# Layer norms applied by ScalarE with scale and bias, and the high half of a transposed mixing rounded straight from PSUM, in a four-layer graph stack

## The reference

```
h = max(layernorm(x), 0);  x = x + L0(h, adj)   # hypergraph: D^-1 H B^-1 H^T (h W1^T) + b1, relu, a layer norm
                                                # over 1024 with gamma and beta, then the same with W2, b2
h = max(layernorm(x), 0);  x = x + L1(h, adj)   # three times adj @ (h W) + b, relu after the first two
h = max(layernorm(x), 0);  x = x + L2(h, adj)   # attention transition T from two scores; relu(sum_k T^k h Wk + bk)
h = max(layernorm(x), 0);  x = x + L3(h, adj)   # relu([h, adj h / degree] W^T)
layernorm(x) = (x - mean) / sqrt(var + 1e-5)
```

## Time and profile before

| | |
|---|---|
| runs | 2774.39 us, median of 3 (2774.32 to 2774.5) |
| profiled execution, span from its first to its last instruction | 2775.4 us |
| around the span | nothing that the profile shows; the median of the runs is 1.0 us shorter |
| PE, PEld busy | 2708.2 us (98%), 2255.6 (81%) |
| DVE, ACT, POOL busy | 2130.3 us (77%), 977.0 (35%), 1219.8 (44%) |
| 16 groups of layer 0, 1, 2, 3 | up to about 945, 1670, 2330 us and the end |

### The profile page before, as it was taken

One profiled execution on the slowest core, in us unless ns is written; L12 is line 12 of the kernel. 1 busy time (PEld: TensorE's weight loads), 2 busy tenths in 40 slices (PEclk: granted clock), 3 DMA queues, 4 the chain that ended last, 5 costly groups with the idle time before them and its releaser, 6 DMA issues.

```text
span 2775.4 us, 42799 instructions
## 1 busy us (share of the span) xinstructions
PE 2708.2 (98%) x13410; PEld 2255.6 (81%) x13410; DVE 2130.3 (77%) x4696; ACT 977.0 (35%) x1905; POOL 1219.8 (44%) x1463
## 2 busy tenths in 40 slices
PE   6999999999999999999999999999999999999999
PEld 4888878888788788888888887888888887888887
DVE  6888888888888766666666668888888887777776
ACT  3334333343333445555554552222222222121221
POOL 4433444343443667677676773211211213333332
PEclk9999999999999999999999999999999999999999
DMA  4111111111111311111111122111111112233232
GB/s 129 41 36 43 38 36 40 36 45 36 36 39 40 95 48 57 41 56 47 51 49 53 49 78 67 53 55 53 53 55 53 53 55 86 87 90 94 80 94 76
DMA packets 126793, 161.26 MB, mean 58 GB/s; under 512 B 53408, under 2 KB 53408, under 8 KB 126752
## 3 DMA queue, kind: packets, MB, share of 16 engines
q1 hardware_dynamic: 121856, 151.84, 17.6%
q10 hardware_dynamic: 4896, 8.92, 1.1%
HBM read 93.60 MB, written 67.11 MB: 58 GB/s over the span
## 4 chain that ended last, share of the span: by engine, by line
PE 84%; DVE 7%; issue 3%; POOL 3%; ACT 2%; DMA 0%; SPq 0%; DVEq 0%; ACTq 0%; POOLq 0%
PE ps L388 25%; PE ps L390 24%; PE ps L389 24%; PE ps L404 4%; PE ps L417 3%; PE ps L406 2%; DVE col_lo L729 1%; DVE normed L756 1%; POOL col_lo L1067 1%; DVE stats L737 1%; DVE wide L875 1%; DVE row_lo L729 1%; ACT row_hi L574 0%; ACT col_hi L574 0%; POOL w_lo L1067 0%
## 5 line engine op out<-in xcount | busy, mean ns | idle before, releaser
L388 PE MATMUL ps<-w_hi,col_hi 128*128 128x512 f32 x3072 | 1233.0, 401 | 24.7 <-DVE col_lo L729 16.3
L390 PE MATMUL ps<-w_hi,col_lo 128*128 128x512 f32 x3072 | 1200.7, 391 | 0.0
L389 PE MATMUL ps<-w_lo,col_hi 128*128 128x512 f32 x3072 | 1197.7, 390 | 0.0
L388 PEld LDWEIGHTS ps<-w_hi,col_hi 128*128 128x128 f32 x3072 | 577.6, 188 | 143.1 <-DVE col_lo L729 24.2
L390 PEld LDWEIGHTS ps<-w_hi,col_lo 128*128 128x128 f32 x3072 | 576.8, 188 | 125.7
L389 PEld LDWEIGHTS ps<-w_lo,col_hi 128*128 128x128 f32 x3072 | 578.9, 188 | 107.0 <-issue 0.2
L1079 POOL TENSOR_TENSOR var_eps<-moments,eps_ln 128x1 f32<-128x1 f32 x256 | 65.2, 255 | 936.5 <-DVE moments L740 935.9
L1067 POOL TENSOR_TENSOR col_lo<-wide,col_hi 128x512 fp32r<-128x512 f32 x192 | 255.8, 1336 | 136.1 <-ACT col_hi L574 136.1
L574 ACT ACTIVATE row_hi<-ps 128x512 fp32r<-128x512 f32 x256 | 152.4, 596 | 429.1 <-PE ps L390 425.9
L729 DVE TENSOR_TENSOR row_lo<-ps,row_hi 128x512 fp32r<-128x512 f32 x256 | 175.3, 685 | 141.0 <-ACT row_hi L574 136.5
L1067 POOL TENSOR_TENSOR row_lo<-normed,row_hi 128x512 fp32r<-128x512 f32 x128 | 169.4, 1329 | 199.6 <-ACT row_hi L574 199.6
(11 more groups left out here) (129 smaller groups left out, 3756.5 us busy)
## 6 DMA issues: line engine op xcount, KB each, us to landing
out<-x_res SPq DMA_DIRECT2D x256, 256.0 KB, 2.0
x_in<-out SPq DMA_DIRECT2D x192, 256.0 KB, 2.7
x_in<-x SPq DMA_DIRECT2D x64, 256.0 KB, 2.6
adj_in<-adj_t SPq DMA_DIRECT2D x96, 64.0 KB, 2.3
raw<-w ACTq DMA_DIRECT2D x12, 256.0 KB, 2.8
raw<-wk ACTq DMA_DIRECT2D x12, 256.0 KB, 2.7
raw<-w0a SPq DMA_DIRECT2D x8, 256.0 KB, 4.3
raw<-w0b SPq DMA_DIRECT2D x8, 256.0 KB, 2.9
```

The lines of the kernel that those rows point to most:

```text
L388: nc.tensor.matmul(out_ap, lhs_hi, rhs_hi, start=start, stop=False)
L389: nc.tensor.matmul(out_ap, lhs_hi, rhs_lo, start=False, stop=False)
L390: return nc.tensor.matmul(out_ap, lhs_lo, rhs_hi, start=False, stop=stop)
```

## The change

Four things change; the lists of steps stay as they are.

- The norms move from DVE's `normalise` to one on ACT: one activation computes relu(`rstd` * x + `shift`) from `x_in` to `normed`. The relu of `split` goes. The mid norm of layer 0 moves to ACT likewise, without a relu.
- POOL makes what the activation needs: `neg_mean` = -mean, and after `rstd` the product `shift` = `neg_mean` * `rstd`; the same for the mid norm.
- In the transposed mixing ACT rounds the first half of PSUM straight to `col_hi`. The copy of the second half and DVE's add go.
- The low part is two DVE operations, `low_part`: first half minus `col_hi` to `wide`, and that plus the second half to `col_lo`. In layer 1 POOL's subtraction goes. DVE has nothing left in the steps `adj0` to `adj2`; its pair stands at `adj0hi` to `adj2hi`. ACT has its rounding at `adj0` to `adj2` and nothing left at the steps with `hi`.

```diff
@@ ACT
+            def normalise(layer, g, t):
+                act.wait_ge(s["shift"], nl(layer, g, t))
...
+                nc.scalar.activation(normed[:, t, :], x_in[:, t, :], ACT.Relu, bias=shift[:, t:t + 1],
+                                     scale=rstd[:, t:t + 1]).then_inc(s["norm"], 1)
             def split(layer, g, t):
                 act.wait_ge(s["norm"], nl(layer, g, t))
-                relu(normed[:, t, :], normed[:, t, :]).then_inc(s["relu"], 1)
-                act.wait_ge(s["relu"], nl(layer, g, t))
...
                 if name == "adj0":
                     act.wait_ge(s0["adj0"], i)
-                    if not first(g):
-                        act.wait_ge(s0["tra"], i - SLOTS)
-                    copy(blocks(wide[:, t, 0:F]), halves(t)[1]).then_inc(s0["adj0_rest"], 1)
-                if name == "adj0hi":
-                    act.wait_ge(s0["adj0_sum"], i)
-                    copy(col_hi[:, t, :], wide[:, t, 0:F]).then_inc(s0["adj0_hi"], 1)
+                    copy(blocks(col_hi[:, t, :]), halves(t)[0]).then_inc(s0["adj0_hi"], 1)
...
+                if name == "midnorm":
+                    act.wait_ge(s0["shift2"], i)
+                    nc.scalar.activation(wide[:, t, :], wide[:, t, :], ACT.Identity, bias=shift2[:, t:t + 1],
+                                         scale=rstd2[:, t:t + 1]).then_inc(s0["norm2"], 1)
@@ DVE
+            def low_part(t, left, left_done, i):
+                V.tensor_tensor(blocks(left), halves(t)[0], blocks(f32(col_hi[:, t, :])), ALU.subtract).then_inc(left_done, 1)
+                dve.wait_ge(left_done, i)
+                return V.tensor_tensor(blocks(col_lo[:, t, :]), halves(t)[1], blocks(left), ALU.add)
...
-                V.tensor_scalar(normed[:, t, :], x_in[:, t, :], moments[:, t, 0:1], rstd[:, t:t + 1],
-                                ALU.subtract, ALU.mult).then_inc(s["norm"], 1)
...
-                if name in ("adj0", "adj1", "adj2"):
-                    dve.wait_ge(s1[name + "_rest"], i)
-                    V.tensor_tensor(blocks(wide[:, t, F:HID]), halves(t)[0], blocks(wide[:, t, F:HID]), ALU.add).then_inc(s1[name + "_sum"], 1)
+                if name in ("adj0hi", "adj1hi", "adj2hi"):
+                    dve.wait_ge(s1[name[:4] + "_hi"], i)
+                    low_part(t, wide[:, t, F:HID], s1[name[:4] + "_left"], i).then_inc(s1[name[:4] + "_lo"], 1)
@@ POOL
+                Q.tensor_tensor(neg_mean[:, t:t + 1], moments[:, t, 0:1], minus_one, ALU.mult)
                 pool.wait_ge(s["var_eps"], nl(layer, g, t))
                 Q.tensor_tensor(rstd[:, t:t + 1], var_eps[:, t:t + 1], half_neg, ALU.pow).then_inc(s["rstd"], 1)
+                pool.wait_ge(s["rstd"], nl(layer, g, t))
+                Q.tensor_tensor(shift[:, t:t + 1], neg_mean[:, t:t + 1], rstd[:, t:t + 1], ALU.mult
+                                ).then_inc(s["shift"], 1)
...
-                if name in ("adj0hi", "adj1hi", "adj2hi"):
-                    pool.wait_ge(s1[name[:4] + "_hi"], i)
-                    lo_of(col_lo[:, t, :], wide[:, t, F:HID], col_hi[:, t, :]).then_inc(s1[name[:4] + "_lo"], 1)
```

More of the change, by code:

```diff
@@ L233, in graph_stack @@
         raw_loaded = [sem(f"raw_loaded{i}") for i in range(RAW)]
-        s = sems("", "adj_loaded rows_loaded stats moments var_eps rstd norm relu resid split_hi split_lo "
+        s = sems("", "adj_loaded rows_loaded stats moments var_eps rstd shift norm resid split_hi split_lo "
                      "final raw_hi raw_lo raw_lo_v raw_scaled cols_loaded vec_loaded b1_loaded wv_loaded "
@@ L243, in graph_stack @@
         s1 = sems("l1_", "asplit_hi asplit_lo " + " ".join(
-            f"adj{c} adj{c}_rest adj{c}_sum adj{c}_hi adj{c}_lo lin{c} bias{c} row{c}_hi row{c}_lo" for c in range(3)))
+            f"adj{c} adj{c}_hi adj{c}_left adj{c}_lo lin{c} bias{c} row{c}_hi row{c}_lo" for c in range(3)))
         s2 = sems("l2_", "s_j s_i s_ib diag tr tr_hi tr_lo lin2 row2_hi row2_lo sj score leak exp alpha s_eps s_inv trans "
@@ L598, in hyper @@
             def hyper(g, name, t, i):
+                if name == "norm":
+                    normalise(0, g, t)
                 if name == "split":
@@ L639, in gcn @@
                     act.wait_ge(s1[name], i)
-                    copy(blocks(wide[:, t, F:HID]), halves(t)[1]).then_inc(s1[name + "_rest"], 1)
-                if name in ("adj0hi", "adj1hi", "adj2hi"):
-                    act.wait_ge(s1[name[:4] + "_sum"], i)
-                    copy(col_hi[:, t, :], wide[:, t, F:HID]).then_inc(s1[name[:4] + "_hi"], 1)
+                    copy(blocks(col_hi[:, t, :]), halves(t)[0]).then_inc(s1[name + "_hi"], 1)
                 if name in ("lin0hi", "lin1hi"):
@@ L649, in diffuse @@
             def diffuse(g, name, t, i):
+                if name == "norm":
+                    normalise(2, g, t)
                 if name == "tr":
@@ L666, in mean @@
             def mean(g, name, t, i):
+                if name == "norm":
+                    normalise(3, g, t)
                 if name == "tr":
@@ L761, in hyper @@
                     statistics(0, g, t)
-                if name == "norm":
-                    normalise(0, g, t)
                 if name == "hprep":
@@ L815, in hyper @@
                                     ).then_inc(s0["dm_sum"], 1)
-                if name == "adj0":
-                    dve.wait_ge(s0["adj0_rest"], i)
-                    V.tensor_tensor(blocks(wide[:, t, 0:F]), halves(t)[0], blocks(wide[:, t, 0:F]), ALU.add
-                                    ).then_inc(s0["adj0_sum"], 1)
                 if name == "adj0hi":
                     dve.wait_ge(s0["adj0_hi"], i)
-                    lo_of(col_lo[:, t, :], wide[:, t, 0:F], col_hi[:, t, :]).then_inc(s0["adj0_lo"], 1)
+                    if not first(g):
+                        dve.wait_ge(s0["tra"], i - SLOTS)
+                    low_part(t, wide[:, t, 0:F], s0["adj0_left"], i).then_inc(s0["adj0_lo"], 1)
                 if name in ("tra", "trb"):
@@ L888, in diffuse @@
                     statistics(2, g, t)
-                if name == "norm":
-                    normalise(2, g, t)
                 if name == "score":
@@ L956, in mean @@
                     statistics(3, g, t)
-                if name == "norm":
-                    normalise(3, g, t)
                 if name == "tr":
@@ L1108, in hyper @@
                         pool.wait_ge(s["vec_loaded"], 64)
-                    pool.wait_ge(s["relu"], i)
+                    pool.wait_ge(s["norm"], i)
                     Q.tensor_tensor(x_res[:, t, :], x_in[:, t, :], normed[:, t, :], ALU.add).then_inc(s["resid"], 1)
```

57 lines of the change are left out of this document (29 added, 28 removed).

## The result

The changed kernel takes 2757.0 us (median of four runs, 2754.7 to 2757.3) against 2774.4 for the kernel before on the same chip: a ratio of 0.9931, 95% interval 0.9919 to 0.9943. The profiled execution has a span of 2755.1 us against 2775.4. The prediction was 2752, with a range of 2737 to 2768. So the time lies 5 us above the predicted value. The sum that led there was wrong in three of its terms for the kernel's parts: by the traces, one error of 14.9 us and two of 6.6 in the other direction, which made up for most of it.

The account below looks back on a forecast made before the run. TensorE was taken as the bound, idle only 1.60 us a group in layer 0 and 0.35 in layer 1. Span 2775.4 - 23 (layer 0) + 0 (layer 1) + 1 (seams) = 2753.4, median 1.0 less: 2752 us, range 2737 to 2768.

Parts of the forecast that it names:

- The first product of slot 3: Layer 0, once a group: TensorE's wait for VectorE's `col_lo`, queued behind the mid norm, goes whole; 1.23 us gained.
- The transposes of slot 1: Layer 0, once a group: TensorE's wait for the mid norm shrinks; 0.3 of 0.42 us gained, bounds 0 and 0.42.
- The pair of slot 0: Layer 0: both VectorE operations now stand behind the residual, so the product starts later; 0.1 us lost, bounds 0 and 0.5.
- Layer 1: Per group, 0.5 us saved at a product and lost at the next mixing: 0, bounds 0.5 gained and 1.7 lost.
- a group grown by over 0.5: Layer 1: a group longer by over half a microsecond would show the prediction wrong.
- the slower rival: VectorE's pairs are stretched to 1110 ns; layer 1 loses 1.7 us per group, 27 in all: 2779; chance 0.06.
- Seams and start: At the three seams between layers, ScalarE's norms delay copies TensorE waits for: 1 us lost, bounds 3 gained, 4 lost.
- From the span to the time: Whole kernel: the median of the runs lies 1.0 us under the profiled span.
- ScalarE's durations: Norms on ScalarE: 625 ns for 512 elements, upper bound 754; mid norm 1.06 us, upper bound 1.28.
- the 23 of layer 0: Layer 0: 1.43 us gained per group, 23 us over 16 groups.

Follow-up runs that it names:

- first_early: The changed kernel with the first operation of the pair one step earlier (adj0 instead of adj0hi) in layer 0 alone: 2748.7 us, ratio 0.9904.
- pool_late: The changed kernel, but in layer 1 GpSimd's subtraction of slot 0's row_lo for the next group waits for VectorE's row_lo of slot 3: 2740.0 us, ratio 0.9869.
- first_norms_dve: The changed kernel, but VectorE applies the four norms of the very first group, at the places where the kernel before had them: 2758.9 us, ratio 0.9941.
- the mixing half: The kernel before with only the transposed mixing as in the changed kernel, the norms staying on VectorE: 2816.9 us, ratio 1.0147.

## Why the prediction was right, and where it was not

- **The first product of slot 3, 1.23.** Right (1.26 with the same matmuls of both traces lined up), and so was its reason, a `col_lo` that no longer queues behind the mid norm. What I had not seen is that neither half of the change does this alone (56.46 and 56.92 against 55.34).
- **The transposes of slot 1, 0.3 of 0.42.** The whole wait went, 0.48, although the mid norm took 1.25 and not 1.06: the chain ahead of it starts earlier, the bias over 1024 columns 6.53 before PE wants the transposes instead of 6.23. A third loss of 0.28 ahead of a mixing (L404 in before) also went; I had not counted it, since it was hidden behind the shown end of the matmul before and PE's list of waits did not have it.
- **The pair of slot 0, -0.1.** Mis-sized: -0.31. The two operations behind L866 take 1.41 together, near the 1.46 that I put, but the residual can have come only some 0.2 earlier against PE, not 0.4 to 0.5; `first_early` won the 0.31 back.
- Together 1.26 + 0.48 + 0.28 - 0.31 = 1.71 of the 1.85 measured, against 1.43 predicted; the rest are differences under 0.1 each.
- **Layer 1, 0 per group, bounds 0.5 gained and 1.7 lost.** This step failed: +0.93. PE's wait moved where the prediction had put it, from the product to the mixing that reads `row_lo` of slot 3. The 0.5 at the product was gained. What it would cost at the mixing was put at the same 0.5, with an operation of 0.66; without the meeting it is 0.33 (`pool_late`), so the chain up to its start was right. But the operation took 1.77, and 1.39 was lost. The price stood in the trace of before, at another slot, where PE did not wait for it (16 of the 128 L879 took that long):

```profile
1435.03 1.29 POOL L1067 TENSOR_TENSOR col_lo<-wide,col_hi 128x512 fp32r<-128x512 f32 x1
...
1435.14 1.73 DVE L879 SCALAR_TENSOR_TENSOR row_lo<-wide,row_hi 128x512 fp32r<-128x512 f32 x1 [0.70 <-ACT row_hi L571]
```

- My bound of 1.7 rested on the right mechanism, a stretched VectorE, but put it on the pair. The pair reads PSUM and one SBUF tile and was never stretched (0.66 to 0.69 in all 512 operations); L885 reads two SBUF tiles. The question "what will the freer engine do earlier, and beside whom" was asked of VectorE and not of GpSimd. The prediction had named a group grown by over 0.5 as what would make it wrong, and for this layer it was.
- The Trainium skill says in "SBUF — State Buffer", Who interferes with whom, that a VectorE instruction with at most one SBUF input, outside its two-port modes, does not contend with GpSimd, and that one with two SBUF inputs contends with a GpSimd instruction that reads SBUF. The trace agrees: 0.68 and 0.69 for the pair, 1.77 for L885. By that rule the slower rival, which stretched the pairs, could have been left out and this meeting looked for.
- **Seams and start, 1 us lost, bounds 3 gained and 4 lost.** Wrong in sign: 5.6 gained by the two traces, outside the bounds, and 2.7 by the medians, just inside. I looked for what ScalarE's norms delay and not for what VectorE's absent ones free; `first_norms_dve` shows the greater part of it, 3.8 at the first product.
- **From the span to the time, 1.0 less.** This was wrong too: the time is 1.8 us over the span in every execution that has both, and the 1.0 came from setting a slower execution's span beside the median. For the span the forecast was 2753.4 against 2755.1 measured, 1.7 off. More than half of the 5 us by which the time was missed is this term.
- **ScalarE's durations.** I took the relu's 625 as the nearest row; 810 was measured, outside the bound of 754. The Trainium skill's figure in "ScalarE: Activation LUTs", What ACT_TABLE_LOAD costs, 93 ns for each pointer operand, was nearer: measured 83 and 99. It did not matter to the sum, since ScalarE had the room.
- The net came near by luck: layer 1's loss of 14.9 was offset by 6.6 more than the 23 of layer 0 and by 6.6 more than the seams' -1.

What stays open: why two of the fifteen groups of layer 1 in the mixing half kept the upper clock through the same pause, what makes the clock fall or stay at the start of layer 2, and where in its trace the kernel before spent the 2.8 us by which that execution was slower than the median.

## What to carry to other kernels

When an edit takes work off one engine and puts it on another, follow the next operations of both: they can move onto each other. Here a meeting of two subtractions cost 1.1 us a group on the path that PE waited for. Two halves of a change should be timed apart and together; one of these lost 1.5% alone and helped in company. The list of waits of the changed kernel named the one place where moving a single step of the order gave more (25 us) than the change itself.

## What the runs showed of the hardware

- A VectorE subtraction that reads two SBUF tiles and starts 0.06 us after a GpSimd one takes 1.77 us instead of 0.69; started 0.47 or 0.48 after, it takes 1.34 or 1.35. In all these cases, and in the 1.73 of the kernel before (0.11 after), it ends 0.54 to 0.56 us after GpSimd's does. The pair's operations, with one operand in PSUM, keep 0.66 to 0.69.
- When VectorE's operation came first, by 0.44 us, it kept its 0.69 and GpSimd's took 1.40 instead of 1.28 to 1.30.
- An ACTIVATE of 128x512 takes 629 ns with constants, 712 with a scale column, 811 with a scale and a bias column.
- In layer 1 of the mixing half, after a pause of 2.05 us in an otherwise full stretch PE ran at its lower clock level for a while in 13 of 15 groups (about seven matmuls of 512 columns in the group shown). In the other two, after 2.02 and 2.05, it did not, nor in the steady groups of the other kernels after 1.39 and 1.23.
